# A four-layer graph network on one core: its indirect row transfers waited for in pairs

## The chip, the cores and the metric

The kernel runs on one core of a Trainium2 chip. The time is device microseconds of that core for one execution. A profiled execution leaves a trace of every instruction and of every transfer's packets; the rows below are from it.

## The reference

The graph has 12500 nodes with 32 features and 200000 edges, sorted by destination. What is computed, cut to what matters here:

```python
h = relu(layernorm(x))
x = x + L0(h, edge_weight, edge_attr, edges)    # per edge: radial weights times h[src] times directions,
                                                # then out.at[dst].add(msg)
h = relu(layernorm(x))
for W, b in ((W1, b1), (W2, b2), (W3, b3)):     # three graph convolutions
    msg = (h @ W)[src] * norm[:, None]
    h = relu(segment_sum(msg, dst) + b)         # self loops among the edges
x = x + h
```

Each of the four sums over edges needs, for every edge, the row of its source node. In layer 0 the row has 32 numbers in float32, in the first and third convolution 96 in bfloat16 (three parts of 32), in the second 128 in float32 (the hidden width).

## The kernel before, in words

Each layer n first writes its node rows to a table in device memory (`tables[n]`). Then the edges are worked off in groups of 1024: `TPG` = 8 tiles of 128 edges. Layer 0 has all of its 196 groups done with gathered rows. The convolutions do only a first part of the edges so (`GATHERED`: 92, 100 and 64 groups); the rest of the edges, in "buckets" of 1408, get their source rows by one-hot matrix products on TensorE from a copy of the table that lies in the core's memory, steered by a table of places that ScalarE loads from device memory for each bucket (`load_places`, line 972). Gathered groups and buckets run side by side in one loop body.

A gathered group works like this. SP loads the 1024 source indices into one of `UNROLL` = 4 index buffers (`load_idx`). POOL (`gathers`, from line 766) waits for the indices and for a free row buffer (four of these as well), and then issues eight indirect transfers, j = 0 to 7, each of which fetches 128 rows of the table by 128 indices (line 785). In layer 0 ScalarE then takes the group's rows (line 884 on) and VectorE and TensorE make messages of them; in a convolution TensorE multiplies the rows with one-hot matrices of the destinations (line 2157) and VectorE adds the sum to the accumulator (line 1770).

What sets the order around the change are semaphores. Each transfer raises a landing semaphore by 16 when its data has landed. There are `LANES` = 4 of these (`gathered`), and transfer j of a group raises number j modulo 4. Before every transfer POOL waits (`wait_landed`, line 755) until the transfer `IN_FLIGHT` = 3 places ahead of it in the stream has landed, so that at most three are in flight. The stream runs on over group and layer boundaries. In the first and last iteration of each layer's loop, which are written out ("peeled"), the awaited count is a constant; in the loop it stands in a register, one for each semaphore (`landed`), which is raised by 16 after each wait. The registers get their starting values at line 810. Those who use the rows wait with `wait_gathered` (line 466) for all lanes: SP before it loads new indices into the buffer, ScalarE in layer 0, TensorE in the convolutions.

POOL does little else: some fills of memory in layer 0, and before the third convolution the subtractions of line 803.

Of the kernel before, what the change touches and what calls it, by code (L numbers as in the profile page):

```python
# [36 lines left out]
TPG = 8  # L37
# [21 lines left out]
MSGW = TAIL0 + OUTS  # L59
SUMW = 8 * OUTS  # L60
PAD_REL = -1000.0
LANES = 4
IN_FLIGHT = 3
assert NG % UNROLL == 0 and PTAIL * KS == ETAIL and PTAIL <= P and NG == 2 * NB


# [2 lines left out]
GATHERED = [NG, 92, 100, 64]  # L69
LOOP = [(UNROLL, 0), (12, 10), (12, 8), (8, 12)]  # L70
# [64 lines left out]
def gnn_kernel(nc, x, src, dst, edge_attr, edge_weight, w1, b1, w2, b2,  # L135
               W1, B1, W2, B2, W3, B3, out):
    ctx = ExitStack()
    with ctx:
# [6 lines left out]
        def sem(name):  # L145
            return ctx.enter_context(nc.semaphore(name))
# [177 lines left out]
        def sems(name, count=UNROLL):  # L324
            return [sem(f"{name}{i}") for i in range(count)]
# [23 lines left out]
        idx_in = [sem(f"idx_in{u}") for u in range(UNROLL)]  # L349
        gathered = sems("gathered", LANES)  # L350
        ew_in = sems("ew_in")
# [101 lines left out]
        def rounds_before(n):  # L453

            return sum(GATHERED[:n]) // UNROLL

        def convs_before(n):
            return sum(GATHERED[1:n]) // UNROLL

        def when(sems, step, event, each=1, before=0):  # L460


            n = len(sems)
            return sems[event % n], step.times(step.groups * each // n, before * (UNROLL * each // n) + event // n + 1)

        def wait_gathered(eng, n, step, u):

            each = 16 * TPG // LANES
            for lane in range(LANES):
                eng.wait_ge(gathered[lane], step.times(step.groups * each, each * (sum(GATHERED[:n]) + u + 1)))  # L470
# [56 lines left out]
        def thirds_before(n):  # L527

            return 0 if n == 1 else len(HALVES)
# [10 lines left out]
        def shape(n, last):  # L540

            groups, buckets = REST[n] if last else LOOP[n]
            return groups, buckets * NCK, [-(-u * buckets * NCK // groups) for u in range(groups)]

        def sweep(eng, body, n=0):

            body(Step(eng, 0, n), True, False)
            with eng.Fori(1, ITS[n] - 1) as it:
                body(Step(eng, it, n), False, False)
            body(Step(eng, ITS[n] - 1, n), False, True)  # L550
# [12 lines left out]
        def blocks_of(c):  # L563
            return slice(c * CH, c * CH + chunks[c][2] // P)

        def chunks_stored(n, c):

            return 16 * (c // 4 + 1) + (16 * len(range(c % 4, NCH, 4)) if n == 3 else 0)
# [163 lines left out]
        @block.gpsimd  # L732
        def _(pool):
            nc.gpsimd.memset(xn[:, NB - 1, :], 0.0).then_inc(pads, 1)
            pool.wait_ge(pads, 1)
            nc.gpsimd.memset(attr_rows[96:NB, 1, :], 1.0).then_inc(pads, 1)
            pool.wait_ge(pads, 2)
            nc.gpsimd.iota(iota_i[:, :], pattern=[[1, WIN]], base=0, channel_multiplier=0).then_inc(made, 1)
            nc.gpsimd.iota(line_i[:, :], pattern=[[0, 1]], base=0, channel_multiplier=1).then_inc(made, 1)
            nc.gpsimd.iota(far_shift_i[:, :], pattern=[[WIN, NB + 1]], base=0, channel_multiplier=0).then_inc(made, 1)  # L740
            nc.gpsimd.memset(ident[:, :], 0.0).then_inc(made, 1)
            nc.gpsimd.memset(one[:, :], 1.0).then_inc(made, 1)
            nc.gpsimd.memset(ew_row[:, :, :], 0.0).then_inc(made, 1)
            nc.gpsimd.memset(idx[:, :, :], 0).then_inc(made, 1)
            nc.gpsimd.memset(ones_h[:, :], 1.0).then_inc(made, 1)
            pool.wait_ge(made, 8)
            nc.gpsimd.affine_select(out=ident[:, :], in_=ident[:, :], compare_op=ALU.not_equal, fill=1.0,
                                    base=0, pattern=[[-1, P]], channel_multiplier=1).then_inc(made, 1)

            turn = [pool.alloc_register(f"turn_pool{u}") for u in range(UNROLL)]
            landed = [pool.alloc_register(f"landed{lane}") for lane in range(LANES)]

            def wait_landed(step, n, u, j):

                lane = (j - IN_FLIGHT) % LANES
                if step.peeled:
                    before = TPG * (sum(GATHERED[:n]) + step.it * step.groups + u) + j - IN_FLIGHT
                    if before >= 0:  # L760
                        pool.wait_ge(gathered[lane], 16 * (before // LANES + 1))
                else:
                    pool.wait_ge(gathered[lane], pool.snap(landed[lane]))  # L763
                    pool.reg_add(landed[lane], landed[lane], 16)  # L764

            def gathers(n):
                def body(step, first, last):
                    for u in range(shape(n, last)[0]):
                        r, use = u % UNROLL, u // UNROLL
                        pool.wait_ge(idx_in[r], step.times(step.groups // UNROLL * 16, 16 * (rounds_before(n) + use + 1)))  # L770
                        if n > 0:
                            if step.peeled and (not first or use):
                                pool.wait_ge(*when(group_summed, step, u - UNROLL, before=convs_before(n)))
                            elif not step.peeled:
                                pool.wait_ge(group_summed[r % 2], pool.snap(turn[r]) + (2 * convs_before(n) + r // 2 + 1))
                                pool.reg_add(turn[r], turn[r], 2)
                        elif last:
                            pool.wait_ge(rows_copied[r], step.it * (step.groups // UNROLL) + use)
                        elif not first:
                            pool.wait_ge(rows_copied[r], pool.snap(turn[r]) + 1)  # L780
                            pool.reg_add(turn[r], turn[r], 1)
                        for j in range(TPG):
                            col = j % 2 * KS + j // 2
                            wait_landed(step, n, u, j)
                            (pool.indirect_dma_start(rows_3[:, r, j, :] if n in (1, 3) else rows[:, r, j, 0:WIDTH[n]], None, tables[n],  # L785
                                                     bass.IndirectOffsetOnAxis(ap=idx[:, r, col:col + 1], axis=0))
                                 .then_inc(gathered[j % LANES], 16))
                    if n == 0 and first:
                        pool.wait_ge(centred, 2)
                        nc.gpsimd.memset(xn[:, NB - 1, :], 0.0).then_inc(pads, 1)  # L790
                        pool.wait_ge(prepared, 1)
                        nc.gpsimd.memset(accT[:, :], 0.0).then_inc(acc_cleared, 1)
                        pool.wait_ge(directed, 1)
                        nc.gpsimd.memset(src_b[:, (NBG - 1) * BJ:NBG * BJ], NO_SOURCE).then_inc(pads, 1)
                        nc.gpsimd.memset(dst_b[:, (NBG - 1) * BJ:NBG * BJ], -1).then_inc(pads, 1)
                if n < 2:
                    pool.wait_ge(table_out[n], 48 if n == 0 else 32)
                else:
                    if n == 3:
                        for c in range(NCH):  # L800
                            bs = blocks_of(c)
                            pool.wait_ge(middle_made, thirds_before(3) + c + 1)
                            nc.gpsimd.tensor_tensor(thirds3[:, bs, 2 * F:F3], lnA[:, bs, :], thirds3[:, bs, F:2 * F],
                                                    ALU.subtract).then_inc(thirds_made, 1)
                    for c in range(NCH - 4, NCH):
                        pool.wait_ge(chunk_out[c % 4], chunks_stored(n, c))
                for u in range(UNROLL):
                    pool.reg_mov(turn[u], 2 * (LOOP[n][0] // UNROLL - 1) if n else 0)
                for lane in range(LANES):
                    pool.reg_mov(landed[lane], 16 * ((TPG * (sum(GATHERED[:n]) + LOOP[n][0]) + lane) // LANES  # L810
                                                     - (1 if lane >= LANES - IN_FLIGHT else 0) + 1))
                sweep(pool, body, n)

            for n in range(NLAYER):
                gathers(n)
# [1471 lines left out]
```

## Time and profile before

| what | value |
|---|---|
| median of 3 runs | 5417.69 us (5406.81 to 5417.71) |
| the profiled execution's own time | 5435.04 us |
| its span, first to last instruction | 5433.2 us |
| PE busy | 4139.9 us (76%) |
| DVE busy | 3579.5 us (66%) |
| POOL busy | 3523.1 us (65%) |
| ACT busy | 2698.1 us (50%) |
| indirect transfers (line 785) | 3616, POOL busy 3496.6 us, idle before them 1799.8 us |

The engines are TensorE (PE, its weight loads PEld), VectorE (DVE), ScalarE (ACT), GpSimd (POOL) and SyncE (SP). Layer 0 runs from about 34 us to 2100, the first convolution from 2165 to 3260, the second from 3296 to 4545, the third from 4595 to the end. The busy time of POOL in an indirect transfer is the time in which it makes the transfer's descriptors; the transfer itself goes on after it. A name after an arrow in a row is what ended an engine's idle time.

### The profile page before, as it was taken

The page shows a single profiled execution, that of the slowest core. Times are in us where ns is not written, and L with a number is a line of the kernel's source. Part 1 is how long each engine was busy: PE and PEld are TensorE (multiplying, and loading weights), DVE is VectorE, ACT ScalarE, POOL GpSimd, SP SyncE. Part 2 cuts the span into 40 slices and gives each one's busy share as a digit, 9 for nine tenths or more (in the row PEclk, how much of TensorE's full clock was granted, in tenths as well). Part 3 has the DMA queues.
Part 4 walks back from the last instruction along what each step waited for, and adds up shares of the span by engine and source line. Part 5 has one row for each costly group of instructions (what it writes and reads, how often), then busy time and mean ns, then how long its engine had stood idle before and what let it go on. Part 6 is the DMA issues. An engine that isn't in the chain of part 4 may idle for free.

```text
span 5433.2 us, 177263 instructions
## 1 busy us (share of the span) xinstructions
PE 4139.9 (76%) x62463; PEld 3114.3 (57%) x62464; DVE 3579.5 (66%) x8469; ACT 2698.1 (50%) x6550; POOL 3523.1 (65%) x3660
## 2 busy tenths in 40 slices
PE   4888888888888886555555558899888998666566
PEld 3555555555555554444444447787777886454444
DVE  8888988888998887766666674333333345554445
ACT  4555555555555554766666654444444445333332
POOL 5777777777777773666666664666666663665554
PEclk9999999999999997555555559999999998666666
DMA  3111111111111114333333324333333333444433
GB/s 92 38 38 38 38 38 38 38 40 39 38 38 38 38 38 44 87 76 79 76 80 78 78 68 130 89 89 94 89 90 92 89 104 108 121 112 114 117 113 105
DMA packets 494971, 400.93 MB, mean 74 GB/s; under 512 B 269575, under 2 KB 454828, under 8 KB 493537
## 3 DMA queue, kind: packets, MB, share of 16 engines
q10 hardware_dynamic: 146996, 207.67, 11.5%
q0 software_dynamic: 115712, 109.02, 10.7%
q1 hardware_dynamic: 231536, 74.48, 6.4%
q8 instruction: 465, 7.62, 0.6%
q14 instruction: 262, 2.15, 0.1%
HBM read 375.52 MB, written 15.29 MB: 72 GB/s over the span
## 4 chain that ended last, share of the span: by engine, by line
DMA 63%; issue 18%; POOL 10%; PE 5%; DVE 2%; POOLq 1%; ACT 0%; DVEq 0%; SPq 0%; ACTq 0%
DMA rows<-table,idx 62%; POOL rows L785 10%; PE radial L2071 2%; POOLq L764 1%; PE psX L2086 1%; PE psT L2086 1%; PE sums L2157 1%; DMA table<-arena 1%; PE radial L2213 0%; POOLq L763 0%; PE radial L2226 0%; DMA xn<-in_x 0%; ACT rows L1107 0%; PE radial L2012 0%; DVE rows L1831 0%
## 5 line engine op out<-in xcount | busy, mean ns | idle before, releaser
L785 POOL DMA_INDIRECT rows<-table,idx x3616 | 3496.6, 967 | 1799.8 <-DMA rows<-table,idx 1074.6
L2071 PE MATMUL radial<-arena,shared 128*32 128x96 bf16 (+1 forms) x31200 | 924.9, 267 | 157.5 <-issue 60.5
L1946 PEld LDWEIGHTS sums<-scratch,onehot 128*64 128x64 f32 x9408 | 795.7, 137 | 400.9 <-DVE scratch L1381 230.0
L1946 PE MATMUL sums<-scratch,onehot 128*64 128x264 f32 (+1 forms) x9408 | 929.4, 341 | 65.9 <-DVE scratch L1381 54.9
L2071 PEld LDWEIGHTS radial<-arena,shared 128*32 128x32 bf16 (+1 forms) x31200 | 664.4, 116 | 294.8 <-issue 80.4
L1011 ACT CAST scratch<-radial 128x480 bf16<-128x480 f32 x860 | 476.5, 555 | 672.6 <-PE radial L2071 665.6
L2157 PE MATMUL sums<-onehot,rows 128*128 128x80 f32 (+1 forms) x2844 | 365.6, 296 | 570.8 <-DMA rows<-table,idx 564.7
L1364 DVE TENSOR_TENSOR scratch<-radial,shared 128x768 f32<-128x768 f32 x784 | 741.6, 946 | 0.0
L1770 DVE TENSOR_TENSOR accT<-accT,sums 96x80 f32 (+1 forms) x256 | 60.3, 236 | 950.0 <-PE sums L2157 949.1
L2157 PEld LDWEIGHTS sums<-onehot,rows 128*128 128x128 f32 (+1 forms) x2844 | 330.2, 206 | 620.4 <-issue 618.6
L1931 PE MATMUL radial<-shared 64*128 64x384 f32 x3136 | 650.6, 492 | 0.0
L854 ACT ACTIVATE dist<-iota,rel 128x64 f32<-128x64 f32 (+1 forms) x2368 | 619.2, 342 | 30.7 <-issue 26.0
L884 ACT COPY shared<-rows 128x192 f32<-128x192 f32 x196 | 88.7, 452 | 933.1 <-DMA rows<-table,idx 931.5
L1356 DVE TENSOR_TENSOR scratch<-radial,shared 128x512 f32<-128x512 f32 x784 | 533.8, 681 | 13.4 <-issue 13.4
L1617 DVE TENSOR_SCALAR shared<-scratch,line 128x640 bf16<-128x640 bf16 (+1 forms) x906 | 418.4, 462 | 168.4 <-PE radial L2071 106.6
L1928 PE MATMUL radial<-shared 64*128 64x384 bf16 x1568 | 267.1, 335 | 271.9 <-DVE scratch L1364 222.5
L1928 PEld LDWEIGHTS radial<-shared 64*128 64x128 bf16 x1568 | 80.7, 93 | 547.5 <-DVE scratch L1364 335.1
L1007 ACT COPY scratch<-radial 128x384 f32<-128x384 f32 x350 | 167.7, 479 | 445.9 <-PE radial L2071 441.9
L1643 DVE TENSOR_TENSOR shared<-iota,shared 128x480 f32<-128x480 f32 x350 | 230.9, 660 | 212.9 <-PE psT L2086 108.1
L1646 DVE TENSOR_TENSOR shared<-radial,shared 128x480 bf16<-128x480 bf16 x860 | 342.9, 400 | 27.9 <-issue 15.0
L1931 PEld LDWEIGHTS radial<-shared 64*128 64x128 f32 x3136 | 289.4, 193 | 3.6 <-issue 3.2
L989 ACT ACTIVATE shared<-scratch,line 128x640 bf16<-128x640 bf16 x304 | 252.2, 829 | 63.2 <-DMA scratch<-places_d 36.0
(236 smaller groups left out, 5537.1 us busy)
## 6 DMA issues: line engine op xcount, KB each, us to landing
scratch<-places_d ACTq DMA_DIRECT2D x242, 800.0 KB
rows<-table,idx POOLq DMA_INDIRECT x3616
shared<-in_edge_weight SPq DMA_DIRECT2D x390, 128.0 KB
idx<-in_src SPq DMA_DIRECT2D x451, 4.0 KB
table<-arena SPq DMA_DIRECT2D x24, 256.0 KB, 2.4
table<-arena SPq DMA_DIRECT2D x2, 1176.0 KB, 10.6
accT<-in_edge_attr SPq DMA_DIRECT2D x2, 1152.0 KB
table<-arena SPq DMA_DIRECT2D x24, 96.0 KB, 2.0
```

The lines of the kernel that those rows point to most:

```text
L785: (pool.indirect_dma_start(rows_3[:, r, j, :] if n in (1, 3) else rows[:, r, j, 0:WIDTH[n]], None, tables[n], bass.IndirectOffsetOnAxis(ap ...
L854: ins = nc.scalar.activation(dist[:, j, 0:span], iota[:, 0:span], ACT.Abs, scale=-1.0, bias=rel[:, bass.ds(step.tile(u) + j, 1)])
L1011: nc.scalar.copy(taken[n][:, h, :, :], radial[0][:, h, 0:KC * F3].rearrange("p (t f) -> p t f", f=F3)).then_inc(bucket_copied, 1)
L1356: prod = v.tensor_tensor(msg[:, h, t:t + 2, 0:2 * SEG0].rearrange("p t (m s) -> p t m s", s=16), R[:, :, 0:256].rearrange("p t (m s) -> p ...
L1364: last = v.tensor_tensor(msg[:, h, t:t + 2, SEG0 + 16 * (MUL + 1):TAIL0].rearrange("p t (n s) -> p t n s", s=16), R[:, :, 256:384].unsquee ...
L1617: v.tensor_scalar(from_src[n][:, k % 2, :, :, :], places[v_ % 2][:, :, c * KC * CAP:(c + 1) * KC * CAP].rearrange("p i (t r) -> p i t r", ...
L1646: v.tensor_tensor(by_twos(to_dst[n][:, k % 2, :, :]), row_pairs(iota1_ps, KC), in_pairs(dst_pair[:, v_ % 2, c * KC:(c + 1) * KC, :], BWIN) ...
L1928: nc.tensor.matmul(radial[q % 2][:, k, 0:RDIM], ones_h[half, :], bias_rows[half, :], start=True, stop=False, tile_position=(k * HID0, 0))
L1931: last = nc.tensor.matmul(radial[q % 2][:, k, 0:RDIM], hid[half, u % 2, q, :], w2n[half, 0, :], start=False, stop=True, tile_position=(k * ...
L1946: last = nc.tensor.matmul(there, onehot[:, u % 2, 4 * h + t, 0:SW], taken_from, start=(h + q + part == 0), stop=(h == 1 and q == 1 and par ...
L2071: last = nc.tensor.matmul(d, from_src[n][:, h, i, t, :], table_of(n, s), start=True, stop=True, tile_position=(0, 32 * i))
L2157: mm = nc.tensor.matmul(sums[0:w, u % 2, 0:CWIN], far_rows[j], (onehot if n == 2 else onehot_3)[0:counts[j], u % 2, j, 0:CWIN], start=(j = ...
```

## The change

The four landing semaphores become two (`LANES`), and `IN_FLIGHT` gives way to `TOGETHER` = 2. The eight transfers of a group form four pairs; both of a pair raise the same semaphore, pairs taking turns between the two. POOL waits only before the first of a pair, until the pair before the last has landed with both transfers (32 counts). `wait_gathered` isn't edited; with two lanes it makes two waits of 64 counts for each group in place of four of 32.

```diff
--- before.py
+++ after.py
@@ -59,8 +59,8 @@
 MSGW = TAIL0 + OUTS
 SUMW = 8 * OUTS
 PAD_REL = -1000.0
-LANES = 4
-IN_FLIGHT = 3
+LANES = 2
+TOGETHER = 2
 assert NG % UNROLL == 0 and PTAIL * KS == ETAIL and PTAIL <= P and NG == 2 * NB
 
 
@@ -754,14 +754,14 @@
 
             def wait_landed(step, n, u, j):
 
-                lane = (j - IN_FLIGHT) % LANES
+                lane = j // TOGETHER % LANES
                 if step.peeled:
-                    before = TPG * (sum(GATHERED[:n]) + step.it * step.groups + u) + j - IN_FLIGHT
+                    before = (TPG * (sum(GATHERED[:n]) + step.it * step.groups + u) + j) // TOGETHER - LANES
                     if before >= 0:
-                        pool.wait_ge(gathered[lane], 16 * (before // LANES + 1))
+                        pool.wait_ge(gathered[lane], 16 * TOGETHER * (before // LANES + 1))
                 else:
                     pool.wait_ge(gathered[lane], pool.snap(landed[lane]))
-                    pool.reg_add(landed[lane], landed[lane], 16)
+                    pool.reg_add(landed[lane], landed[lane], 16 * TOGETHER)
 
             def gathers(n):
                 def body(step, first, last):
@@ -781,10 +781,11 @@
                             pool.reg_add(turn[r], turn[r], 1)
                         for j in range(TPG):
                             col = j % 2 * KS + j // 2
-                            wait_landed(step, n, u, j)
+                            if j % TOGETHER == 0:
+                                wait_landed(step, n, u, j)
                             (pool.indirect_dma_start(rows_3[:, r, j, :] if n in (1, 3) else rows[:, r, j, 0:WIDTH[n]], None, tables[n],
                                                      bass.IndirectOffsetOnAxis(ap=idx[:, r, col:col + 1], axis=0))
-                                 .then_inc(gathered[j % LANES], 16))
+                                 .then_inc(gathered[j // TOGETHER % LANES], 16))
                     if n == 0 and first:
                         pool.wait_ge(centred, 2)
                         nc.gpsimd.memset(xn[:, NB - 1, :], 0.0).then_inc(pads, 1)
@@ -807,8 +808,7 @@
                 for u in range(UNROLL):
                     pool.reg_mov(turn[u], 2 * (LOOP[n][0] // UNROLL - 1) if n else 0)
                 for lane in range(LANES):
-                    pool.reg_mov(landed[lane], 16 * ((TPG * (sum(GATHERED[:n]) + LOOP[n][0]) + lane) // LANES
-                                                     - (1 if lane >= LANES - IN_FLIGHT else 0) + 1))
+                    pool.reg_mov(landed[lane], 16 * TPG * (sum(GATHERED[:n]) + LOOP[n][0]) // LANES)
                 sweep(pool, body, n)
 
             for n in range(NLAYER):
```

## Rows read from the trace of the kernel before

**Rows 1.** The page's chain that ended last, by engine.
```profile
DMA 63%; issue 18%; POOL 10%; PE 5%; DVE 2%; POOLq 1%; ACT 0%; DVEq 0%; SPq 0%; ACTq 0%
```

**Rows 2.** The chain by line: layer 0, then first, second, third convolution.
```profile
by line: DMA rows<-table,idx 73.1%; issue 17.5%; POOL rows L785 8.1%; POOLq L764 1.1%; POOLq L763 0.2%; POOLq L781 0.0%; POOLq L548 0.0%; POOLq L780 0.0%; POOLq L761 0.0%
...
by line: DMA rows<-table,idx 68.1%; issue 18.8%; POOL rows L785 11.6%; POOLq L764 0.9%; POOLq L763 0.3%; POOLq L776 0.2%; POOLq L775 0.1%; POOLq L761 0.0%; POOLq L548 0.0%; POOLq L770 0.0%
...
by line: DMA rows<-table,idx 50.2%; issue 23.8%; POOL rows L785 11.3%; PE radial L2071 5.4%; PE psX L2086 2.8%; PE psT L2086 2.7%; PE sums L2157 2.1%; POOLq L764 0.7%; POOLq L763 0.5%; POOLq L776 0.3%; POOLq L775 0.1%; POOLq L548 0.1%; PE p
...
by line: DMA rows<-table,idx 72.8%; issue 16.6%; POOL rows L785 9.8%; POOLq L764 0.9%; POOLq L763 0.4%; POOLq L776 0.1%; POOLq L775 0.0%; POOLq L761 0.0%; POOLq L770 0.0%
```

**Rows 3.** Timeline, POOL: start us, duration us, what, [idle before <- releaser].
```profile
35.03 0.94 POOL L785 DMA_INDIRECT rows<-table,idx  x1 [0.30 <-issue]
```

**Rows 4.** Groups by line, L785, same four stretches: xcount | busy, mean | idle.
```profile
L785 POOL DMA_INDIRECT rows<-table,idx x1490 | 1423.2, 955 | 507.7 <-DMA rows<-table,idx 374.5 <-issue 133.2
...
L785 POOL DMA_INDIRECT rows<-table,idx x704 | 680.9, 967 | 360.7 <-DMA rows<-table,idx 235.4 <-issue 125.3
...
L785 POOL DMA_INDIRECT rows<-table,idx x773 | 764.9, 989 | 405.3 <-DMA rows<-table,idx 222.1 <-issue 183.2
...
L785 POOL DMA_INDIRECT rows<-table,idx x481 | 459.8, 956 | 301.7 <-DMA rows<-table,idx 210.6 <-issue 91.1
```

**Rows 5.** Timeline, POOL: a stop, and the one 110 issues later.
```profile
1059.69 0.94 POOL L785 DMA_INDIRECT rows<-table,idx  x1 [3.04 <-issue]
...
1201.77 0.94 POOL L785 DMA_INDIRECT rows<-table,idx  x1 [2.35 <-issue]
```

**Rows 6.** The chain in order of time: start us, us, what (first convolution).
```profile
2370.70 5.51 DMA rows<-table,idx
...
2387.29 5.96 DMA rows<-table,idx
...
2395.26 2.43 DMA rows<-table,idx
```

**Rows 7.** Timeline, ScalarE's queue: issues of the place tables' loads.
```profile
2370.12 0.41 ACTq L972 DMA_DIRECT2D scratch<-places_d  x1
...
2386.66 0.41 ACTq L972 DMA_DIRECT2D scratch<-places_d  x1
```

**Rows 8.** Timeline, POOL, same stretch: issues beside these loads.
```profile
2373.70 0.95 POOL L785 DMA_INDIRECT rows<-table,idx  x1 [0.80 <-DMA rows<-table,idx]
2376.97 0.95 POOL L785 DMA_INDIRECT rows<-table,idx  x1 [2.32 <-DMA rows<-table,idx]
...
2390.27 0.94 POOL L785 DMA_INDIRECT rows<-table,idx  x1 [0.70 <-issue]
2394.01 0.94 POOL L785 DMA_INDIRECT rows<-table,idx  x1 [2.80 <-DMA rows<-table,idx]
2395.26 0.95 POOL L785 DMA_INDIRECT rows<-table,idx  x1 [0.30 <-issue]
```

**Rows 9.** Waits of SP's queue, layer 0: us in total, times, longest.
```profile
SPq L470 <- DMA rows<-table,idx: 1515.8, 371, 9.5
```

**Rows 10.** Busy time by stretch; after the bracketed counts: PEclk, DMA share, GB/s.
```profile
130.00:2060.00 1930.00, 1649.58 (x13594) 1061.33 (x13594) 1730.26 (x3352) 1021.79 (x2981) 1422.35 (x1490) 0.99 0.19 39
2200.00:3240.00 1040.00, 613.57 (x15030) 494.26 (x15029) 692.08 (x2330) 669.83 (x1063) 679.63 (x704) 0.55 0.31 80
3320.00:4490.00 1170.00, 1063.83 (x18014) 944.62 (x18016) 431.79 (x818) 527.02 (x1579) 764.73 (x773) 0.93 0.33 93
4630.00:5390.00 760.00, 469.81 (x11743) 372.10 (x11743) 377.94 (x1261) 251.26 (x450) 459.00 (x481) 0.68 0.41 116
```

**Rows 11.** TensorE's waits for the rows, first, second, third convolution.
```profile
PE sums L2157 <- DMA rows<-table,idx: 220.3, 81, 7.4
...
PE sums L2157 <- DMA rows<-table,idx: 86.0, 41, 5.1
...
PE sums L2157 <- DMA rows<-table,idx: 250.3, 61, 8.8
```

## The prediction

> **What bounds the kernel now.** I read the chain of waits first, then the same chain cut to the four layers, then the page's busy times by stretch, and last the single issues of POOL in order of time. Over the whole span 63% of the chain is transfers on their way, and most of the rest is "issue" and POOL [rows 1]; the transfers are nearly all `rows<-table,idx`, the indirect ones of line 785. Cut to the layers [rows 2], transfers, issue and POOL together hold over 98% of the chain in layer 0 and in the first and third convolution, but only some 85% in the second, where TensorE's matmuls hold a good part of the rest. So what ends last is the stream of 3616 indirect transfers, with one stretch in which TensorE shares that place.
>
> That stream has a floor and stalls above it. The second issue of the program has nothing to wait for, and still starts 0.30 us after the first has ended; it takes 0.94 us [rows 3]. A wait that is already met thus costs nothing: the floor is about 0.95 + 0.30 = 1.25 us per transfer with or without it. The stalls are POOL's idle time before line 785 [rows 4] less 0.303 us per issue: 507.7 - 1490 x 0.303 = 56 us in layer 0, 360.7 - 704 x 0.303 = 147 in the first convolution, 405.3 - 773 x 0.303 = 171 in the second, 301.7 - 481 x 0.303 = 156 in the third; 530 us in these four stretches. They are not all landings: once in 110 issues there is a stop of 2 to 3 us that the landing of the transfer three places back doesn't explain; one stands in [rows 5], with its fellow 110 issues later. 33 of these, at some 2 us, are 66 us, and the change doesn't touch them. About 465 us are left as waits for landings.
>
> **How a stall is made.** A transfer lands 2.43 us after its issue began when nothing is in the way, and 5.51 or 5.96 us when something is [rows 6]: the load of a place table for the whole core (line 972) was issued 0.6 us before each of these two [rows 7]. The issue that waits for a landing starts 0.75 us behind it: 2370.70 + 5.51 = 2376.21, next start 2376.97; 2387.29 + 5.96 = 2393.25, next start 2394.01 [rows 6, 8]. With three in flight, issue k is late as soon as k - 3 takes longer than 3 x 1.25 - 0.75 = 3.0 us.
>
> **The change, part by part.** A pair waits for both transfers of the pair before the last. For the first of a pair (even k) that means k - 3, as now, and k - 4, for which k - 1 waits now. The second of a pair (odd k) waits for nothing. So no wait is later than today's as long as transfers take as long as today; in flight are at most four at an odd k, three at an even one. The loop's starting counts (line 810) give 16 x 8 x groups / 2 on both semaphores, which is what the written-out iterations ask for too, so the relaxation holds everywhere.
>
> Removed, at one answer each: half the waits and register additions on POOL (0, since the 0.30 us gap is there without them [rows 3]); two of four waits per group in `wait_gathered` on SP, ScalarE and TensorE (0: what they wait for is the eighth transfer's landing, and SP stands in that wait for 1515.8 us of layer 0's 1930 [rows 9]). If the cover of POOL's 0.95 us per issue were gone, each wait left would cost its 0.75 us; that cover stays. Behind a waiting POOL stand only further transfers and, before the third convolution, line 803's subtractions. No instruction moves to another queue.
>
> The gain is in the odd stalls. Two cases stand in [rows 8]. The issue at 2376.97 is the fifth of its group, even: it waits for the same landing after the change, and its 2.32 us stay; the odd issue ahead of it at 2373.70 wins 0.5 us, which are waited out there. The issue at 2394.01 is the eighth, odd: it would start at the floor, 2390.27 + 0.94 + 0.30 = 2391.51. The next one, even, then meets the landing at 2393.25 and can start at 2394.01 at the earliest; now it starts at 2395.26. That is up to 1.25 us won, less what its second transfer lands later than the first.
>
> I rolled both rules forward over all 3616 issues (first to last, with their own durations): start = the later of the previous end + 0.30 and the awaited landing + 0.75 (0.26 in the iterations written out, where the count is a constant), all other stops kept. A landing is known where a stall shows it. Where none does, it lies between 2.40 us after issue and the latest that would not have stalled. With the early end the change gives 169 us (25 in layer 0, 59, 41 and 45 in the convolutions), with the late end 11 us. The quiet landing of [rows 6] is at 2.43, so I stay near the early end; but a transfer beside a late one is late as well, which takes a part of the 1.25 us above. I take 150: **layer 0 25, then 48, 35 and 42**.
>
> What of it reaches the end? In layer 0 VectorE is next: it is busy for 1730 of 1930 us [rows 10], so 25 us fit. In the first and third convolution TensorE is busy 614 of 1040 and 470 of 760 us and waits 220 and 250 us for these rows [rows 10, 11]: 48 and 42 count whole. In the second it is busy 1064 of 1170 us and waits 86 us: I count half of 35, 17, since in half of its groups TensorE, not the transfer, is late. Sum: 25 + 48 + 17 + 42 = 132 us. Against the profiled execution's 5435.0 us that is 5303; the median of the runs is 17.4 us lower, so **5285 us**, 2.4% under 5417.7.
>
> **A rule that speaks against it.** The short landings with one or two others in flight show no queueing, and the transfer engines are busy for a share of 0.31 to 0.41 in the convolutions [rows 10]; it is only behind a table load that they are full. The Trainium skill ("DMA: Bandwidth & Descriptors", section "Issuing engines are not separate DMA queues") says that transfers of whatever engine run on the same 16 DMA engines and interleave. By that rule alone a fourth transfer behind a table load takes its time from the other three, and the gain would go to zero or below; the trace has no case of four in flight, so it is neither borne out nor refuted.
>
> **The rivals.**
> 1. *The stall only moves on.* Late landings come so spread out that the even issue stalls for nearly all that the odd one saved: near the late end, 11 to 70 us, say 40: 5378 us. Against it: the odd issue of 2394.01 is followed by one with no further stall. For it: 2373.70 and 2376.97 stall in a row [rows 8]. Chance 0.12.
> 2. *The fourth transfer slows the others, slower than before.* Its place is the few us behind a table load, where line 785's issues already land at 5.5 to 6 us. If it adds 0.3 us to each late landing the 169 us fall to 82, at 0.5 to 21, and at 0.7 the stream is 43 us longer: it decides from 0.57 us on, and 0.7 gives 5461 us. Against it: the extra transfer starts when the first of its fellows is 3.7 us old, and it is 128 rows beside a whole place table. Chance 0.07.
> 3. *Another bound takes over:* VectorE in layer 0 and TensorE in the second convolution take all of 25 + 17 us: 90 us are left, 5328 us. Within the forecast's range.
> 4. *No effect* (another limit on what POOL may have under way, such as the one behind the stop in 110, already holds at three): 5418 us, chance 0.05. That the edit doesn't do what it says I exclude by the counts above.
>
> **How the numbers follow.** The forecast with rival 3 has 0.76: 70 to 183 us, from rival 3 with a fifth off, to the early end's 169 and 14 more for matters that I set to zero. Range 5235 to 5390: its upper end takes in most of rival 1; left out are rivals 2 and 4 and the outermost of rival 1, some 0.15. A measurement of this kernel can tell about 0.2%, 11 us. Faster: 0.76 + 0.11 = 0.87, less a little: 0.86. Within 0.2%: 0.05 + 0.01 = 0.06. Slower: 0.08.
>
> **What would show it.** After the change POOL's idle before line 785 should fall from 507.7, 360.7, 405.3 and 301.7 by about 25, 48, 35 and 42; odd issues should all start 0.30 us after the one before, save the stops in 110; quiet landings should still take 2.4 us and late ones 4 to 6; TensorE's wait for rows in the first and third convolution should fall by the same amounts, in the second by half. I am wrong if late landings grow past 6.5 us, if even stalls grow by what the odd ones lose, or if the second convolution doesn't move while VectorE's idle in layer 0 is gone.

## The result, and the profile after

The changed kernel takes 5262.38 us (median of 4 runs, 5255.4 to 5268.67) against 5417.35 for the kernel before (4 runs beside them): a ratio of 0.9714 [0.97, 0.9728], or 155 us less. The profiled execution took 5268.67 us, with a span of 5266.9.

The page of the changed kernel, its chain by engine and the row of the indirect transfers (line 786 now):

```profile
DMA 55%; issue 18%; POOL 16%; PE 7%; DVE 2%; POOLq 1%; ACT 0%; DVEq 0%; SPq 0%; ACTq 0%
...
L786 POOL DMA_INDIRECT rows<-table,idx x3616 | 3493.9, 966 | 1635.5 <-issue 964.0
```

Against [rows 1], transfers hold 55% of the chain where they held 63, and POOL's own work 16 where it held 10. The stream still ends last, but more of it is now POOL's own work on the issues. POOL's busy time is what it was; its idle time before these issues fell from 1799.8 to 1635.5 us. By stretch, in the order of [rows 4]:

```profile
L786 POOL DMA_INDIRECT rows<-table,idx x1491 | 1428.2, 958 | 478.6 <-issue 279.3 <-DMA rows<-table,idx 199.3
...
L786 POOL DMA_INDIRECT rows<-table,idx x708 | 689.6, 974 | 311.4 <-issue 181.2 <-DMA rows<-table,idx 130.2
...
L786 POOL DMA_INDIRECT rows<-table,idx x773 | 757.5, 980 | 357.9 <-issue 208.9 <-DMA rows<-table,idx 147.5 <-PE sums L2157 1.5
...
L786 POOL DMA_INDIRECT rows<-table,idx x484 | 460.2, 951 | 266.6 <-DMA rows<-table,idx 138.4 <-issue 128.2
```

Less 0.303 us per issue these are 27, 97, 124 and 120 us of stalls, where the same sum gave 56, 147, 171 and 156 before: 29, 50, 47 and 36 won. The same stretches by engine (us, PE, PEld, DVE, ACT and POOL busy, then PEclk, DMA share, GB/s), to be held against [rows 10]:

```profile
130.00:2035.00 1905.00, 1656.13 (x13641) 1066.32 (x13639) 1734.96 (x3360) 1023.12 (x2987) 1426.72 (x1491) 0.99 0.19 39
2170.00:3170.00 1000.00, 612.47 (x15130) 492.46 (x15122) 693.98 (x2339) 672.88 (x1068) 688.91 (x708) 0.56 0.33 83
3250.00:4365.00 1115.00, 1043.30 (x18088) 924.75 (x18077) 431.53 (x821) 528.29 (x1586) 757.08 (x773) 0.96 0.34 97
4500.00:5225.00 725.00, 474.39 (x11760) 373.70 (x11758) 381.45 (x1265) 251.47 (x452) 458.66 (x484) 0.68 0.42 122
```

The work is the same in each; only the stretches are shorter. In the second convolution TensorE's busy time fell too, at a higher granted clock (0.96, before 0.93). TensorE's waits for the rows, first to third convolution, as in [rows 11]:

```profile
PE sums L2157 <- DMA rows<-table,idx: 174.4, 68, 6.4
...
PE sums L2157 <- DMA rows<-table,idx: 56.4, 30, 5.2
...
PE sums L2157 <- DMA rows<-table,idx: 184.7, 55, 5.8
```

One late landing of the changed kernel, for comparison with [rows 6 to 8]. The load of a place table, from ScalarE's timeline (start us, us, what):

```profile
2339.23 0.41 ACTq L972 DMA_DIRECT2D scratch<-places_d  x1
```

The transfer issued behind it, from the chain in order of time (start us, us, what):

```profile
2339.76 5.42 DMA rows<-table,idx
```

The issues that follow, from POOL's timeline (start us, us, what, [idle before <- releaser]):

```profile
2342.26 0.94 POOL L786 DMA_INDIRECT rows<-table,idx  x1 [0.30 <-issue]
2345.94 0.94 POOL L786 DMA_INDIRECT rows<-table,idx  x1 [2.74 <-DMA rows<-table,idx]
2347.19 0.95 POOL L786 DMA_INDIRECT rows<-table,idx  x1 [0.30 <-issue]
2348.44 0.94 POOL L786 DMA_INDIRECT rows<-table,idx  x1 [0.30 <-issue]
```

By the chain the late one is the second of its pair; both raise one semaphore and count as landed together. The pair after it goes out at the floor, behind it; then the first of the next pair stands still until 2339.76 + 5.42 + 0.76 = 2345.94, and the ones behind it run at the floor again. One late landing, one stall.

By stage, from its first indirect issue to that of the next (the last to the span's end):

| stage | before, us | after, us | won | forecast |
|---|---|---|---|---|
| layer 0 | 2131.3 | 2101.0 | 30 | 25 |
| first convolution | 1131.1 | 1088.3 | 43 | 48 |
| second convolution | 1298.7 | 1239.5 | 59 | 17 |
| third convolution | 838.4 | 802.3 | 36 | 42 |

### The profile page after: what moved, and what is told of

Read it like the earlier page. It is cut to its first block, busy times and chain, and to the rows that moved or that the text cites. A ratio compares the mean times of both kernels' runs of the same rounds, so it can differ in the third digit from the quotient of the medians.

```text
span 5266.9 us, 173315 instructions
## 1 busy us (share of the span) xinstructions
PE 4119.8 (78%) x62463; PEld 3091.7 (59%) x62464; DVE 3579.8 (68%) x8469; ACT 2695.8 (51%) x6550; POOL 3520.4 (67%) x3660
## 4 chain that ended last, share of the span: by engine, by line
DMA 55%; issue 18%; POOL 16%; PE 7%; DVE 2%; POOLq 1%; ACT 0%; DVEq 0%; SPq 0%; ACTq 0%
DMA rows<-table,idx 55%; POOL rows L786 16%; PE radial L2071 2%; PE sums L2157 1%; PE psT L2086 1%; PE psX L2086 1%; POOLq L764 1%; DMA table<-arena 0%; PE radial L2213 0%; PE radial L2226 0%; DMA xn<-in_x 0%; PE radial L2012 0%; DVE rows L1831 0%; ACT rows L1107 0%; POOLq L776 0%
## 5 line engine op out<-in xcount | busy, mean ns | idle before, releaser
L786 POOL DMA_INDIRECT rows<-table,idx x3616 | 3493.9, 966 | 1635.5 <-issue 964.0
L2157 PE MATMUL sums<-onehot,rows 128*128 128x80 f32 (+1 forms) x2844 | 349.7, 287 | 441.6 <-DMA rows<-table,idx 427.6
L2157 PEld LDWEIGHTS sums<-onehot,rows 128*128 128x128 f32 (+1 forms) x2844 | 314.6, 198 | 490.9 <-issue 488.4
L2089 PE MATMUL psX<-shared,scratch 128*96 128x96 bf16 x2150 | 244.7, 266 | 49.1 <-DVE shared L1646 43.8
```

The costliest lines, as they stand in the source:

```text
L2157: mm = nc.tensor.matmul(sums[0:w, u % 2, 0:CWIN], far_rows[j], (onehot if n == 2 else onehot_3)[0:counts[j], u % 2, j, 0:CWIN], start=(j = ...
```

## The experiments

The theory, A, is depth: the change wins because up to four transfers are under way where three were, so that half of the issues no longer wait for the third one back. Against it stand B, that the waits themselves cost and there are half as many; and C, that a further transfer slows its fellows and takes part of the gain back. Later runs ask what made the second convolution win so much (A2, E), what makes landings late (D, G, H), and whether two semaphores are worth anything beside four (F). "Over the floor" below is POOL's time between issues less 0.304 us each, over all issues of a stage; before it is 82, 148, 174 and 158 us.

**Depth alone, one at a time.** The kernel before with one number changed: every transfer waits for the one four places back.

```diff
-IN_FLIGHT = 3
+IN_FLIGHT = 4
```

> Four lanes as before, one wait ahead of every transfer, but for the transfer four places back instead of three. Theory A (what the odd issues win is depth: a late landing stalls POOL only once the transfers behind it are used up, and how long a landing takes doesn't depend on how many are under way): every issue wins what only the odd ones won. Rolled forward with the landings of the kernel before, the waits for landings fall from 466 us to about 96, the stream is 34 us shorter in layer 0 and 107, 115 and 108 in the convolutions; with TensorE taking back some 30 of the second that is about 5080 us, well under the pairs' 5262. Theory B (the pairs win because POOL has half the waits and register additions): as many waits as before, so 5417 us. Theory C (a fourth transfer takes its time from the others): landings behind a table load grow by 0.5 us and more, and the time is 5262 us or above.

Measured: 5062.26 us, ratio 0.9342 [0.9322, 0.9362]. With as many waits as before and never more than four in flight, it wins 350 us, more than twice the change. Over the floor it has 31, 38, 64 and 47 us.

**The change's rule with the waits and semaphores of before.** Before the first of a pair the kernel waits on two of the four semaphores, so it has as many waits as before.

```diff
-IN_FLIGHT = 3
+IN_FLIGHT = 4
...
-                            wait_landed(step, n, u, j)
+                            if j % 2 == 0:
+                                wait_landed(step, n, u, j)
+                                wait_landed(step, n, u, j + 1)
```

> The pairs' rule with everything else as before: four semaphores, one for each transfer, and two waits with two register additions ahead of the first of a pair (for the transfers four and three places back), none ahead of the second. Theory A: the same issues are free, so the same time as the pairs, 5262 us within 0.3%; POOL's idle time as after the change. Theory B: waits, additions and semaphores are as many as before the change, so 5417 us, or at least half of the way back (5340).

Measured: 5279.99 us, ratio 0.9756 [0.973, 0.9782]. Most of the gain is there without a wait less, so B can't be the main cause.

**The same pairs with `IN_FLIGHT` left at 3.** Half of the issues wait for nothing, and the others for transfers only two and three places back.

> Stops as rare as with pairs, but no more than three in flight: four semaphores, ahead of the first of a pair POOL waits for the transfers three and two places back, ahead of the second for nothing. Theory A: the even issue now waits for a transfer only 2.5 us old, so also quiet landings (2.4 us and 0.75 us behind them) stall it, by some 0.65 us for each pair: rolled forward, layer 0 is 580 us longer and the convolutions 270, 310 and 210, about 6700 us, less where TensorE gives slack. Theory B: half of the stops are gone, so no slower than before, 5260 to 5420 us.

Measured: 6588.07 us, ratio 1.217 [1.2142, 1.2199]. POOL's timeline in the second convolution shows the pairs: one issue at the floor, one that stands still.

```profile
2906.19 0.94 POOL L787 DMA_INDIRECT rows<-table,idx  x1 [0.30 <-issue]
2908.32 0.94 POOL L787 DMA_INDIRECT rows<-table,idx  x1 [1.18 <-DMA rows<-table,idx]
2909.56 0.94 POOL L787 DMA_INDIRECT rows<-table,idx  x1 [0.31 <-issue]
2911.44 0.94 POOL L787 DMA_INDIRECT rows<-table,idx  x1 [0.94 <-DMA rows<-table,idx]
```

An ordinary landing of 2.4 us is already too late for an issue that waits for the transfer two places back. It is as much as A asks for, and a little less than the rolled-forward stream said: free odd issues are worth nothing if the even ones wait for younger transfers.

**Twice the depth.** The changed kernel with four semaphores in place of two: a pair waits for the pair four before it, and up to eight transfers are in flight.

```diff
-LANES = 2
+LANES = 4
```

> Pairs on four semaphores in place of two: a pair is issued when the pair four before has landed, up to eight in flight. Theory A: landings (up to 6.5 us) never hold POOL, the stream goes to its floor of 1.25 us per issue plus the stops once in some 110 issues: 41 us off layer 0 and 131, 144 and 143 off the convolutions against the kernel before, of which TensorE takes back some 50 in the second: about 5010 us. TensorE's granted clock in the second convolution rises from 0.93 to 0.98 or more, as its waits for rows end. Theory C (transfers under way together slow one another): landings grow with depth and the time stays near 5262, or the stops become longer because more must be drained.

Measured: **4940.73 us** (4929.19 to 4943.36), ratio 0.9121 [0.9103, 0.914]. It is 322 us faster than the changed kernel, and 122 us faster than the one-at-a-time rule with four in flight. It is also some 70 us below what A asked for: layer 0 alone won 68 us (2131.3 to 2063.4) where 41 were expected, since the stops that A kept are gone there. Its page's chain and the row of the transfers:

```profile
DMA 43%; POOL 26%; issue 19%; PE 9%; DVE 2%; POOLq 1%; ACT 0%; DVEq 0%; SPq 0%; ACTq 0%
...
L786 POOL DMA_INDIRECT rows<-table,idx x3616 | 3497.7, 967 | 1283.9 <-issue 1008.2
```

One load of a place table, from ScalarE's timeline:

```profile
2346.22 0.41 ACTq L972 DMA_DIRECT2D scratch<-places_d  x1
```

POOL's timeline behind that load:

```profile
2347.17 0.94 POOL L786 DMA_INDIRECT rows<-table,idx  x1 [0.30 <-issue]
2348.41 1.53 POOL L786 DMA_INDIRECT rows<-table,idx  x1 [0.30 <-issue]
2350.25 0.94 POOL L786 DMA_INDIRECT rows<-table,idx  x1 [0.30 <-DMA rows<-table,idx]
2351.50 1.05 POOL L786 DMA_INDIRECT rows<-table,idx  x1 [0.30 <-issue]
```

The second convolution by engine (columns as above):

```profile
3100.00:4140.00 1040.00, 1014.64 (x18134) 898.42 (x18135) 433.32 (x824) 530.97 (x1596) 771.00 (x784) 0.99 0.36 105
```

TensorE's wait for the rows in that stretch (us in total, times, longest):

```profile
PE sums L2157 <- DMA rows<-table,idx: 6.3, 13, 0.5
```

Nothing stalls behind the load any more. Over the floor the four stages have 12, 1, 31 and 0 us: outside the second convolution the stream runs at 1.26 to 1.28 us per transfer, and what bounds it now is POOL's own work on an issue; in the second it is TensorE, whose busy time is 1015 of 1040 us. The chain still books 43% to transfers, but hardly any of that is waiting: by the landing records the awaited pair had landed 1.8 us or more before the issue in all of 1804 cases but one.

These runs settle C as well. How long a pair takes to land, from the start of its second transfer to the later of the two landings (median, then the value that 95% stay under, us), worked out from each trace's landing records, of which 2 to 4% are missing:

| kernel, most in flight | first conv. | second conv. | third conv. |
|---|---|---|---|
| before, 3 | 2.61, 4.57 | 2.74, 4.98 | 3.27, 5.09 |
| the change, 4 | 2.61, 4.61 | 2.72, 4.78 | 3.27, 5.03 |
| one at a time, 4 | 2.81, 4.75 | 2.84, 4.84 | 3.25, 5.17 |
| pairs, 8 | 2.78, 4.78 | 2.70, 4.77 | 3.30, 5.16 |

With eight under way these figures are at most 0.21 us above those with three, where C asked for 0.5 and more. The rule of the Trainium skill that I weighed ("DMA: Bandwidth & Descriptors", section "Issuing engines are not separate DMA queues") says that the transfers of all engines share the 16 DMA engines and interleave; here that sharing costs up to eight such transfers no more than these 0.21 us, the DMA share being 0.50 at most in the fastest kernel's stretches.

**The second convolution alone, and all but it.** The pairs' rule on four semaphores, for `n == 2` alone; the other run has `n != 2`. (`wait_landed` gets the number of places back as an argument, and the starting counts of line 810 follow it.)

```diff
-                            wait_landed(step, n, u, j)
+                            if n == 2:
+                                if j % 2 == 0:
+                                    wait_landed(step, n, u, j, 4)
+                                    wait_landed(step, n, u, j + 1, 4)
+                            else:
+                                wait_landed(step, n, u, j)
```

> The pairs' rule (on four semaphores) in the second convolution alone, the rule of before in the other three layers. In the change's trace the second convolution is 59 us shorter, where 17 had been forecast. Theory A2 (TensorE's own time falls there as well: each of its waits for rows is followed by a stretch at half clock, and fewer waits leave it 0.96 of the full clock instead of 0.93): the gain is the second convolution's own, 45 to 60 us, so 5357 to 5370 us, with the granted clock of the convolution at 0.95 or above. Rival E (the surplus comes from outside, from how the other layers hand over, or is spread between executions): 15 to 35 us, 5380 to 5400 us, clock near 0.93.

Measured: 5380.58 us, ratio 0.9954 [0.9937, 0.997], or 27 us won.

> The reverse: the pairs' rule in layer 0 and in the first and third convolution, the rule of before in the second. Theory A2: 31 + 43 + 36 = 110 us less than before, 5305 us, and the second convolution as long as before (1299 us) at a clock of 0.93. Rival E: the second convolution is shorter too, or the sum of this and of the kernel with the second alone falls short of the 150 us of the whole by over 30.

Measured: 5314.86 us, ratio 0.9827 [0.9811, 0.9843], or 93 us won. The two add up to 120 us, against 132 and 113 for the rule in all layers (the run above and its repeat below). The second convolution of the first of them, with the rule there:

```profile
3318.00:4438.00 1120.00, 1050.39 (x18064) 929.99 (x18052) 432.51 (x820) 527.06 (x1580) 761.45 (x773) 0.95 0.34 97
```

The same of the second, where that layer keeps the rule of before:

```profile
3247.00:4403.00 1156.00, 1068.75 (x18116) 947.83 (x18116) 433.43 (x823) 530.13 (x1587) 762.84 (x775) 0.94 0.33 94
```

With the rule TensorE is busy for 18 us less at a higher granted clock, as after the change, and from its first issue to the next stage's first the layer takes 1248.3 us in place of 1284.2: 36 us. As many are gone from POOL's stalls there, 126 us over the floor in place of 162. So the part of TensorE's clock, on which A2 rests, is there; but by the time of the whole program the layer's gain is the smaller one, of the size that E gave. The 59 us between the profiles of before and after are more than this rule alone brings.

**The place tables' loads cut to a tenth.** The loads of line 972 move a tenth of each piece (80 KB for 800, in as many pieces) from the second iteration of each convolution on.

```diff
+                some = KB * CAP if step.peeled and step.it == 0 else KB * CAP // 10
-                act.dma_start(places[v % 2],
+                act.dma_start(places[v % 2][:, :, 0:some],
...
-                              .rearrange("(i s) -> i s", i=4)[:, 0:KB * CAP].partition_broadcast(P)
+                              .rearrange("(i s) -> i s", i=4)[:, 0:some].partition_broadcast(P)
```

In the kernel before:

> The kernel before, but from the second iteration of each convolution on each load of a place table moves a tenth of the bytes (80 KB in place of 800); the rest of the table keeps what an earlier load left, so the bucketed edges' messages are not computed rightly. Theory A (late landings are those issued beside these loads): landings in the convolutions stay near 2.4 to 3 us, POOL's waits for landings there fall from 134, 146 and 145 us to under 30 each, and only the stops once in 110 issues are left; layer 0 is as before; about 5050 us. Rival D (the landings are late for another reason: the rows' own traffic, the index loads, device memory): less than 60 us are won, 5360 us or more.

Measured: 5239.22 us, ratio 0.9694 [0.9678, 0.971]. Over the floor 83, 80, 104 and 76 us: in the convolutions 259 us where 480 were. Of the 259, 34 stand before every 110th issue, where the stops come.

In the changed kernel:

> The changed kernel with the same cut to the place tables' loads (the same messages left out). Theory A: with no late landings there is little for the pairs to win in the convolutions: 25 to 50 us less than the kernel of before with the same cut, most of it in layer 0 (30 us) and in shorter stops. Rival D, and theory B (fewer waits): the pairs win some 150 us here too.

Measured: 5105.80 us, ratio 0.9442 [0.9426, 0.9458]. Over the floor 49, 53, 60 and 60 us. With small loads the pairs still win 133 us, where 155 were won with full ones. Layer 0, which has no such loads, gives 34 us of stalls; in the convolutions the pairs take away 86 us of them, against 134 with full loads. So neither reading holds as it was put: the loads make about half of what late landings cost (D said much less), and the pairs still win a good part on the other half (A, in its form that late means beside a load, falls).

**A quarter of the pieces as well.** In the kernel before the loads are 20 KB, with 128 pieces in place of 512, to see whether the other half hangs on the number of pieces (G) or on something else (H).

```diff
-                act.dma_start(places[v % 2],
+                quarters, some = (4, KB * CAP) if step.peeled and step.it == 0 else (1, KB * CAP // 10)
+                act.dma_start(places[v % 2][:, 0:quarters, 0:some],
```

> The kernel before with still smaller loads of the place tables: from the second iteration of each convolution on, a quarter of the pieces and a tenth of each piece's bytes (20 KB and 128 pieces for each load, where the first cut left 80 KB in 512 pieces); the bucketed edges' messages are not computed rightly. The first cut took away half of the waits above the floor (147 to 80, 174 to 104, 158 to 76 us). Theory G (what is left of them hangs on the number of pieces of these loads): they fall again by half or more, to under 40, 60 and 40 us, and the time to 5150 us or less. Rival H (the rest has other causes, index loads and the stops): they stay within 15 us of 80, 104 and 76, and the time within 30 us of 5239.

Measured: 5193.27 us, ratio 0.9662 [0.9637, 0.9686]; over the floor 70, 70, 95 and 76 us. The convolutions' 259 us became 241, but layer 0, where nothing was changed, differs by 13 us too, and the intervals of the two ratios meet. So G fails: the pieces count for little or nothing. What makes the other landings late stays open.

**Two semaphores against four, side by side.** The changed kernel as it is, and the pairs' rule on four semaphores once more, on one chip in five rounds.

> The changed kernel as it is, beside the one with four semaphores on the same chip, since the two stood at ratios of 0.9714 and 0.9756 when they were measured apart. Theory A (depth alone): both the same within 0.2%. Theory F (the two semaphores themselves are worth something: half of the register additions on POOL, half of the waits of SP, ScalarE and TensorE): the changed kernel is 15 to 25 us faster than the one with four semaphores here too, 0.3 to 0.5%.

> The pairs' rule on four semaphores, a second time, on the same chip as the changed kernel. Theory A: a ratio within 0.002 of the changed kernel's. Theory F: 0.003 to 0.005 above it.

Measured: 5228.28 us, ratio 0.9729 [0.9712, 0.9745], and 5260.52 us, ratio 0.9782 [0.9758, 0.9806]. The intervals don't meet, so the two semaphores are worth about 0.5%, 32 us here (F asked for 15 to 25). By stage the profiles differ by -1, -8, +33 and +7 us (four semaphores less two): the difference sits in the second convolution. That stretch with two semaphores:

```profile
3246.00:4338.00 1092.00, 1028.42 (x18026) 911.77 (x18021) 430.85 (x818) 525.20 (x1576) 755.42 (x771) 0.97 0.33 99
```

And with four:

```profile
3238.00:4363.00 1125.00, 1050.98 (x18047) 931.11 (x18049) 433.40 (x820) 527.22 (x1582) 758.77 (x773) 0.95 0.32 97
```

For the same matmuls TensorE is busy for 23 us more with four semaphores, at a lower granted clock. POOL's stalls over the floor are longer too, 136 us in place of 104, which is nearly all of the layer's 33 us. What makes them longer was not isolated. The profiles of the first two runs of these rules are 123 and 134 us over the floor in that layer and 14 us apart in its time, so the size of the difference isn't steady.

## Why the prediction was right, and where it was not

**What bounds the kernel, and how a stall is made: right.** Ranked by the youngest landing that an issue waits for, the kernels fall in order: k - 2 (even issues) 6588 us, k - 3 (all) 5412, k - 3 (even only) 5262 and 5280, k - 4 (all) 5062, k - 7 (even only) 4941. Fewer waits and semaphores at the same depth make some 0.5% (the side-by-side runs), and the landings take as long as before.

**The odd issues start at the floor: right.** Of the changed kernel's odd issues 32 start more than 0.8 us behind the last, all of them the stops that I left out of the sum. Counted over all issues, odd stalls fell from 309 to 64 us and even ones grew from 253 to 331. So rival 1's mechanism is there, at a third of its size: of 245 us saved at odd issues, 78 are waited out at the even ones. What is left, 167 us, is the early end of my bound (169); I took 150. One part of it I had left out: I said that the change doesn't touch the stops, but in layer 0 POOL idles at the 13 stops for 1.95 us on average where it was 2.48, which is 7 of the 33 us that layer 0 won over the floor.

**Stalls by stretch.** I said 25, 48, 35 and 42; the rows give 29, 50, 47 and 36. TensorE's waits for the rows fell by 46 and 66 us in the first and third convolution, against the 48 and 42 expected; the third stage got 36 us shorter all the same, so there its other waits took up the rest. Layer 0 won 30 for 25, and VectorE still idles for 1905 - 1735 = 170 us of its stretch: that cover held, and rival 3 had no part.

**The term that was mis-sized: the second convolution's 17 us,** "half of 35". The profiles give 59. It had two wrong halves. The stalls shrank by 47 in the stretch (by 51 over the whole layer), not 35. And I took TensorE's 1064 busy us as fixed, so that a transfer that comes sooner would win only where TensorE stands still. TensorE's timeline of the kernel before, around one of its waits, shows that this isn't so:

```profile
3518.91 1.30 PE L2071 MATMUL radial<-arena,shared 128*32 128x128 f32 x40
3523.49 3.70 PE L2157 MATMUL sums<-onehot,rows 128*128 128x80 f32 x16 [3.27 <-DMA rows<-table,idx]
3526.97 2.31 PE L2086 MATMUL psX<-scratch,shared 128*96 128x128 f32 x10
...
3538.00 2.01 PE L2157 MATMUL sums<-onehot,rows 128*128 128x80 f32 x16
```

The stretches ahead of that wait, behind it and after (columns as above):

```profile
3512.90:3519.70 6.80, 6.80 (x138) 5.97 (x141) 4.05 (x8) 3.34 (x9) 5.28 (x6) 1.00 0.26 59
3522.30:3529.10 6.80, 5.61 (x26) 5.51 (x26) 0.70 (x2) 0.00 (x0) 3.78 (x5) 0.50 0.20 46
3530.00:3555.00 25.00, 24.53 (x457) 21.54 (x449) 10.76 (x22) 13.38 (x40) 17.44 (x18) 1.00 0.29 78
```

TensorE waits 3.27 us for rows, and in the stretch that begins towards the end of this wait the granted clock is 0.50 (1.2 GHz) where it was 1.00 (2.4 GHz): the same 16 matmuls take 3.70 us in place of 2.01. On TensorE's side this late landing is paid for twice. In the layer's stretch of [rows 10] the granted clock fell so 26 times, each time behind or within an idle of TensorE, 21 times one that the rows ended. The Trainium skill ("TensorE: Matmul & The Clock Gate", section "Part 1: The HAM clock gate") says that the clock is set by how busy TensorE has been, between these two levels; the rows agree, with 0.50 behind the wait and 1.00 around it. In this layer the time at 0.50 fell from 154 to 96 us with the change (26 stretches before, 16 after). TensorE's mean matmul went from 1063.83 / 18014 = 59.1 to 1043.30 / 18088 = 57.7 ns, which over the 18088 is 25 us; its wait for rows fell by another 30. Together they are 55 of the 59.

POOL's stream gives the same 59 from its own side. From the layer's first issue to the next layer's, POOL's work on the 800 issues fell from 791 to 784 us, the stalls over the floor from 174 to 123, and what follows the last issue stayed at 90 us. POOL hardly waits for TensorE here (1.5 us in the row of the changed kernel above), so these stalls are waits for landings, and what they lost reached the end whole, with nothing to halve: TensorE kept up, since its own time shrank as well. Whether it would have kept up at the old clock was not tested.

How much of the 59 is the change's own is less sure than the profiles make it look. The run with the rule in that layer alone won 27 us on four semaphores; two semaphores in place of four won 32 more side by side. That the two add up to 59 may be chance: this layer took 1299 us in one profile under the old rule and 1284 in another.

**A step that I set to nothing: half the waits and the semaphores.** The side-by-side runs put 32 us on it, nearly all in the second convolution. In the iterations written out an issue with one constant wait starts 0.26 us behind the landing, one with two waits 0.74; at some 30 such stalls in that layer this could be 15 us. But those iterations hold only 6 of the 31 us of stalls that lie between the two kernels there (26 us with two semaphores, 32 with four). The rest is in the loop, where an issue starts 0.75 us behind the landing with one register as with two: 75 stalls are 61 us with two semaphores, 83 are 91 us with four. So the lag isn't the cause, and why the landings are waited out longer stays open.

**"Only behind a table load": half wrong.** The loads cut to a tenth took away 46% of the convolutions' stalls, from 480 to 259 us; cutting the pieces as well brought nothing clear of the noise. What makes the rest late isn't known. The sum didn't hang on this, since it was made from the landings and not from their cause.

**Rival 2: refuted.** It needed 0.57 us on each late landing; the table of landings shows 0.04 us at most for the change and 0.21 with eight in flight. **Rival 4** is refuted by the deeper kernels.

So 132 us were forecast and 155 measured, 168 between the two profiles' stages: 115 in the three stages where only the stream counts came out as 109, and the surplus is the second convolution's.

## What to carry to other kernels

When a stream of transfers is paced by waits on its own earlier landings, write down for each issue which landing it waits for at the latest, and set the depth by late landings (here 5 to 6 us), not by quiet ones (2.4 us): depth won 472 us here, and grouping waits, some 0.5% aside, only as far as it made the stream deeper. Try the greatest depth that the buffers allow before refining the rule. Where the consumer is TensorE, look at the granted clock behind its waits as well as at the waits, and count the half-clock stretches that stand there.

## What the runs showed of the hardware that was not expected

**A stop of POOL, counted in issues.** The chain of the kernel before in order of time, at the stop of [rows 5]:

```profile
1056.32 3.15 issue
```

A stop of the changed kernel, on POOL's timeline:

```profile
1061.24 1.51 POOL L786 DMA_INDIRECT rows<-table,idx  x1 [1.84 <-issue]
```

For 3.15 us nothing is issued, and the profile knows no releaser. It comes every 110 issues in the kernel before, in the run that waits for the fourth back and in that with `IN_FLIGHT` left at 3 (where 110 issues take 173 us and not 142), so it goes by issues and not by time; in the changed kernel it comes every 112. In the 6 us around the stop shown no packet of an instruction queue was moved. POOL idles for 1.84 to 2.06 us at a stop in layer 0 of the changed kernel and mostly for 1.0 to 1.2 where every issue waits for the fourth back; with eight in flight a single odd issue of 1808 idles for more than 0.8 us. The deeper the stream, the less of it is seen. What it is, the trace doesn't say.

**The lag behind a landing.** An issue whose awaited count stands in a register starts 0.75 us behind the landing, one with a constant 0.26 us behind it; with two waits, one after the other, it is 0.75 us with registers as well, and 0.74 us with constants (medians over the stalled issues of each kernel).
